# A two-layer attention kernel: one side's key transposes moved from TensorE to VectorE and DMAs, with a new written order

## What is computed

```python
# layer 0: attention, then an MLP
xn, yn = layernorm(x), layernorm(ctx)
q, (k, v) = xn @ Wq, split(yn @ Wkv)                 # 16 heads of 16
x = x + softmax(q k^T * hd**-0.5) v @ Wproj + bproj
x = x + gelu(layernorm(x) @ W1 + b1) @ W2 + b2
# layer 1: the last attention
q = rope(rmsnorm(x) @ wq);  k, v = split(ctx @ wkv);  k = rope(k)
q, k = q / norm(q), k / norm(k)                      # per head
return x + softmax(q k^T * hd**0.5) v @ wout
```

## Time and profile before

| | |
|---|---|
| time, median of 3 runs | 341.33 us (341.09 to 341.97) |
| the profiled execution: its own time | 343.29 us |
| the profiled execution: span | 341.5 us |
| busy: TensorE, VectorE, ScalarE, GpSimd | 97%, 78%, 68%, 57% |
| mean granted TensorE clock | 0.992 |

### The profile page before, as it was taken

How to read it: one execution, slowest core, us unless ns; L and a number is a source line. 1 busy time by engine, 2 the same in 40 slices (tenths; PEclk the granted TensorE clock), 3 DMA queues, 4 the chain that set the end, 5 groups by cost and what they waited for, 6 DMA issues and landing times.

```text
span 341.5 us, 10106 instructions
## 1 busy us (share of the span) xinstructions
PE 330.3 (97%) x3929; PEld 295.5 (87%) x3929; DVE 266.7 (78%) x586; ACT 230.6 (68%) x422; POOL 193.2 (57%) x200
## 2 busy tenths in 40 slices
PE   7899999999999999999999999999998999999995
PEld 7877876888778887899999999999998998888884
DVE  2969989988998669778788788666579989887643
ACT  3568876787775653885736665655678867789871
POOL 3585675886542202635857987493662799647100
PEclk9899999999999999999999999999999999999998
DMA  5667411110020000100000010000000000010101
GB/s 155 200 207 234 138 33 31 33 34 2 3 94 2 3 3 2 33 3 0 3 31 2 0 33 3 31 2 32 2 2 0 3 2 33 17 36 33 50 33 63
DMA packets 13007, 13.79 MB, mean 40 GB/s; under 512 B 1440, under 2 KB 12192, under 8 KB 12960
## 3 DMA queue, kind: packets, MB, share of 16 engines
q1 hardware_dynamic: 12240, 12.34, 11.4%
q10 hardware_dynamic: 720, 0.80, 0.8%
HBM read 11.04 MB, written 2.10 MB: 38 GB/s over the span
## 4 chain that ended last, share of the span: by engine, by line
PE 81%; DVE 6%; issue 4%; POOL 3%; ACT 2%; DMA 1%; ACTq 1%; POOLq 0%; DVEq 0%
PE banks_s L1326 12%; PE bank_y L1121 5%; PE banks_s L1216 5%; PE banks_s L1234 4%; PE banks_s L1393 4%; PE bank_o L1121 4%; PE bank_t L1337 4%; PE bank_y L1337 3%; PE bank_t L1121 3%; PE bank_o L1135 2%; PE bank_y L1135 2%; PE bank_o L1266 2%; PE bank_qk L1337 2%; PE bank_o L1337 2%; DVE row_max L2233 2%
## 5 line engine op out<-in xcount | busy, mean ns | idle before, releaser
L436 POOL TENSOR_TENSOR norm_q_inv<-norm_q_min,minus_half 128x32 f32<-128x32 f32 x8 | 43.8, 5476 | 21.0 <-DVE norm_q_min L2416 19.4
L424 POOL TENSOR_TENSOR norm_k_inv<-norm_k_min,minus_half 128x32 f32<-128x32 f32 x8 | 44.5, 5566 | 12.8 <-DVE norm_k_min L2383 12.7
L659 ACT ACTIVATE PT<-banks_s 128x1024 f32<-128x1024 f32 x32 | 31.0, 1023 | 15.7 <-PE banks_s L1243 15.7
L2233 DVE TENSOR_REDUCE row_max<-banks_s 128x8 f32<-128x1024 f32 x32 | 37.6, 1218 | 4.3 <-PE banks_s L1216 4.0
L703 ACT ACTIVATE W_s<-banks_s,small_t 128x256 f32<-128x256 f32 x60 | 25.2, 471 | 20.1 <-PE banks_s L1326 20.0
L1326 PE MATMUL banks_s<-lnT_hi,W_hi 128*128 128x256 f32 x120 | 34.4, 287 | 0.0
L1326 PE MATMUL banks_s<-lnT_hi,W_lo 128*128 128x256 f32 x120 | 33.9, 283 | 0.0
L1326 PE MATMUL banks_s<-lnT_lo,W_hi 128*128 128x256 f32 x120 | 33.9, 283 | 0.0
L685 ACT ACTIVATE PT<-banks_s 128x1024 f32<-128x1024 f32 x32 | 31.2, 1024 | 3.6 <-PE banks_s L1393 3.6
L712 ACT ACTIVATE hT_hi<-W_s 128x512 fp32r<-128x512 f32 x32 | 20.0, 632 | 15.8 <-PE bank_y L1337 10.1
L389 POOL TENSOR_TENSOR x_all<-x_all,b_row 128x256 f32<-128x256 f32 x16 | 12.4, 794 | 27.2 <-DVE b_xn L2316 25.4
(11 more groups left out here) (375 smaller groups left out, 1088.6 us busy)
## 6 DMA issues: line engine op xcount, KB each, us to landing
x_all<-in_x SPq DMA_DIRECT2D x16, 128.0 KB, 2.2
ctx_in<-in_ctx_wide SPq DMA_DIRECT2D x16, 128.0 KB, 2.5
W_s<-in_L_xattn_W SPq DMA_DIRECT2D x2, 1024.0 KB, 7.8
ctx_in<-in_ctx_T SPq DMA_DIRECT2D x8, 256.0 KB, 2.6
out<-x_all SPq DMA_DIRECT2D x16, 128.0 KB, 1.7
W_s<-in_L_xattn_Wq ACTq DMA_DIRECT2D x1, 256.0 KB, 3.4
W_s<-in_L_xattn_Wkv ACTq DMA_DIRECT2D x1, 256.0 KB, 4.5
W_s<-in_L_xattn_Wkv ACTq DMA_DIRECT2D x2, 128.0 KB, 4.8
```

The costliest lines, as they stand in the source:

```text
L424: nc.gpsimd.tensor_tensor(norm_k_inv[:, :], norm_k_min[:, :], minus_half[:, :], ALU.pow).then_inc(c_kinv, 1)
L436: nc.gpsimd.tensor_tensor(norm_q_inv[:, :], norm_q_min[:, :], minus_half[:, :], ALU.pow).then_inc(c_qinv, 1)
L659: nc.scalar.activation(PT[:, t % 2, 2 * h:2 * h + 2, :], banks_s[:, 2 * h:2 * h + 2, :], ACT.Exp, scale=HD ** -0.5).then_inc(a_exped, 1)
L2233: v.tensor_reduce(row_max[:, 8 * h:8 * h + 8], banks_s[:, 2 * h:2 * h + 2, :].rearrange("p n (r k) -> p (n r) k", k=TOK), AX.X, ALU.max).t ...
```

## The change

1. `keys_T` is gone from TensorE. `keys_blocks` on VectorE transposes each 32x32 square of `rot_k` in one instruction of 128x512 into `key_blocks`, and `move_keys` on SP issues 16 DMAs, each of which takes the squares of one block row and one block column (32 partitions, 4 runs of 128 bytes in each) to their places in `keys_in`. Both tiles lie in `wkv_s`, whose weights have been split by then. `keys_out` and `keys_out_lo` read `keys_in` (SBUF) where they read a bank. `keys_turns(p)` waits for `keys_blocks(p - 1)`, `keys_blocks(p)` for the DMAs of pair p - 1.
2. SP's program: `load_context` runs two pairs ahead of `move_keys`; the stores stand behind all of it.
3. The last tile's end is done in two halves of 8 heads: `out_T_half`, `back_half`, `heads_half`, `normed_half`, `out_hi_half`, `out_lo_half`, `project_half`. `weighted_first(31)` and `weighted_second(31)` write different banks.
4. The three DMAs of `Wkv` are issued by SP behind the first four tile loads, no longer by ScalarE's queue.
5. The written order of all four engines is a new one, with other banks for many results. TensorE turns the first pair after `a_bq`; one more idle transpose stands before `queries_a(0)`.

```diff
@@ SP
             load_ctx(1)
+            sp.dma_start(Wkv_s[:, 0, :], Wkv[0:128, :]).then_inc(wkv_loaded, LOADED)
+            for half in (slice(0, C2B), slice(C2B, 128)):
+                sp.dma_start(Wkv_s[half, 1, :], Wkv[128:C2, :]).then_inc(wkv_loaded, LOADED)
             sp.wait_ge(wkv_loaded, 3 * LOADED)
...
+            def move_keys(p):
+
+                sp.wait_ge(c_kblocks, p + 1)
+                wait(sp, c_keys_lo, p)
+                for a in range(4):
+                    blocks = key_blocks[32 * a:32 * a + 32, :].rearrange("p (n b r) -> p b n r", n=4, b=4)
+                    for b in range(4):
+                        to = keys_in[32 * b:32 * b + 32, :].rearrange("p (n a r) -> p a n r", n=4, a=4)
+                        sp.dma_start(to[:, a], blocks[:, b]).then_inc(c_kmoved, LOADED)
+
+            load_context(0)
+            load_context(1)
             for p in range(NP):
-                load_context(p)
+                if p + 2 < NP:
+                    load_context(p + 2)
+                move_keys(p)
@@ ScalarE
-            def keys_out(p, bank):
-
-                act.wait_ge(c_kT, p + 1)
-                nc.scalar.activation(keysT[:, 0, :, of_pair(p)], joined(bank[:, :]), ACT.Copy).then_inc(c_keys, 1)
+            def keys_out(p):
+
+                act.wait_ge(c_kmoved, 16 * LOADED * (p + 1))
+                nc.scalar.activation(keysT[:, 0, :, of_pair(p)].rearrange("p k (j n) -> p k j n", j=2), keys_in.rearrange("p (j k n) -> p k j n", j=2, k=KT), ACT.Copy).then_inc(c_keys, 1)
@@ TensorE
-            def keys_T(p, bank):
-
-                pe.wait_ge(c_kunit, p + 1)
-                turned_pair(bank, rot_k).then_inc(c_kT, 1)
+            def back_half(h, bank):
+
+                pe.wait_ge(oT_ready, 2 * NB + h)
+                for g in (2 * h, 2 * h + 1):
+                    last = nc.tensor.transpose(bank[:, 128 * g:128 * g + 128], oT[:, 128 * g:128 * g + 128], ident[:, :])
+                last.then_inc(o_back, 1)
+
+            def normed_half(h, bank):
+
+                pe.wait_ge(on_ready, 2 * NB + h)
+                nc.tensor.transpose(bank[:, in_pair(h, TOK)], on[:, in_pair(h, TOK)], ident[:, :]).then_inc(on_transposed, 1)
+
+            def project_half(h, bank):
+
+                pe.wait_ge(onT_lo, 2 * NB + h)
+                for n, (x, y) in enumerate(HI_LO):
+                    last = mm(bank[:, 0:C1], onT_r[:, x, h, :], wout_r[:, y, h, :], start=h == n == 0, stop=h == 1 and n == 2)
+                if h == 1:
+                    last.then_inc(proj_mm, 1)
@@ VectorE
+            def keys_blocks(p):
+
+                dve.wait_ge(c_kunit, p + 1)
+                wait(dve, c_kmoved, 16 * LOADED * p)
+                v.transpose(key_blocks[:, :], rot_k).then_inc(c_kblocks, 1)
```

More of the change, by code:

```diff
@@ new lines, in _ @@
+            pe.wait_ge(c_x_lo, 2)
+            queries_c(1, bank_o)
+            down_b(2, 1, 1, bank_qk)
+            pe.wait_ge(b_gelu, 15)
+            up_b(3, 3, bank_s[0])
+            down_b(2, 1, 2, bank_qk)
+            pe.wait_ge(c_krope, 8)
+            turn_b(4, bank_t)
+            down_b(2, 0, 3, bank_y)
+            down_b(2, 1, 3, bank_qk)
+            pe.wait_ge(c_qrope, 4)
+            keys_c(4, bank_o)
+            pe.wait_ge(b_x, 5)
+            inputs_c(2, bank_y)
+            pe.wait_ge(b_gelu, 16)
@@ L2656, in _ @@
-            res_b(1, 1, bank_y)
             hidden_lo(2, 0)
             hidden_lo(2, 1)
+            res_b(1, 0, bank_qk)
+            queries_units(0)
             hidden_lo(2, 2)
+            keys_out_lo(1)
+            res_b(1, 1, bank_o)
+            inputs_lo(1, bank_o)
+            keys_units(2)
             hidden_lo(2, 3)
-            inputs_lo(1, bank_y)
-            keys_turned(2)
-            keys_sums(2)
-            queries_units(0)
+            hidden_lo(3, 0)
+            keys_blocks(2)
@@ L2680, in _ @@
[L2680 to L2687 removed]
+            split_lnT(4, bank_t)
+            res_b(2, 0, bank_y)
+            res_b(2, 1, bank_qk)
+            centre_b(5)
+            hidden_lo(3, 2)
+            normalise_b(5)
+            inputs_lo(2, bank_y)
+            stats_b(6)
+            hidden_lo(3, 3)
@@ L2707, in _ @@
             keys_units(4)
-            res_b(4, 1, bank_y)
+            normalise_b(7)
+            keys_out_lo(3)
+            res_b(4, 1, bank_t)
+            keys_blocks(4)
             hidden_lo(5, 3)
-            keys_out_lo(4, bank_o)
-            keys_turns(5, bank_y)
+            hidden_lo(6, 0)
+            split_lnT(7, bank_t)
+            keys_turns(5, bank_qk)
+            hidden_lo(6, 1)
             keys_turned(5)
             keys_sums(5)
-            split_lnT(7, bank_o)
-            hidden_lo(6, 0)
@@ L2716, in _ @@
-            hidden_lo(6, 1)
-            res_b(5, 0, bank_t)
+            res_b(5, 0, bank_o)
             hidden_lo(6, 2)
+            res_b(5, 1, bank_y)
+            keys_out_lo(4)
+            hidden_lo(6, 3)
             keys_units(5)
-            keys_out_lo(5, bank_o)
-            keys_turns(6, bank_t)
-            res_b(5, 1, bank_y)
-            hidden_lo(6, 3)
+            keys_blocks(5)
+            queries_out_lo(0, bank_o)
+            queries_out_lo(1, bank_y)
+            inputs_lo(3, bank_o)
@@ L2743, in _ @@
-            heads_out(16, bank_o)
-            keys_turns(7, bank_qk)
-            out_lo(16, bank_o)
-            queries_units(2)
-            queries_sums(3)
-            heads_out(17, bank_o)
+            heads_out(17, bank_qk)
+            queries_turns(4, bank_t)
+            keys_units(6)
+            inputs_lo(5, bank_qk)
+            keys_blocks(6)
+            queries_out_lo(2, bank_y)
+            queries_turned(4)
+            res_b(7, 0, bank_o)
+            queries_sums(4)
+            residual(16, bank_y)
@@ L2759, in _ @@
[L2759 to L2774 removed]
+            inputs_lo(6, bank_y)
@@ L2775, in _ @@
+            queries_turns(5, bank_t)
+            residual(17, bank_o)
+            out_lo(18, bank_y)
+            queries_units(4)
+            keys_out_lo(6)
+            residual(18, bank_o)
+            heads_out(19, bank_qk)
+            queries_turned(5)
+            queries_sums(5)
+            keys_units(7)
+            out_lo(19, bank_o)
+            keys_blocks(7)
+            queries_turns(6, bank_y)
+            heads_out(20, bank_qk)
             inputs_lo(7, bank_o)
-            out_lo(19, bank_t)
@@ L2788, in _ @@
-            out_lo(21, bank_t)
+            queries_out_lo(5, bank_t)
+            out_lo(21, bank_o)
+            keys_out_lo(7)
             heads_out(22, bank_qk)
```

1668 lines of the change are left out of this document (819 added, 849 removed).

## The result

| | before | changed |
|---|---|---|
| median of four runs each, us | 341.33 (341.09 to 341.97) | 347.93 (347.08 to 348.55) |
| ratio to before, 95% interval | 1 | 1.0188 (1.0162 to 1.0215) |
| profiled execution: span, us | 341.5 | 345.3 |
| its own time, us | 343.29 | 347.08 |

The change costs 6.4 us by the ratio; I had forecast 3.5 us of gain and a range up to 341.8. It lies where rival B was, outside the range.

A forecast was written before the change was run, and what follows sets the result against it. TensorE's own issue was taken as the bound from about 30 to about 330 us. Terms -3.5 + 0.3 + 0.1 + 0.5 - 0.5 - 0.4 = -3.5 us gave a median of 337.8 us, range 334.8 to 341.8.

The forecast's parts named there:

- rival B: Moves slower than their room, at `keys_out` on ScalarE; pitch over 0.6, at 0.65 +8 us, so 345.8; chance 0.15.
- TensorE's 32 transposes away: Eight groups of four `keys_T` transposes removed from TensorE, 0.44 us a group, all on the path: -3.5 us.
- VectorE's 8 transposes: Eight added 128x512 instructions at 0.69 us, 5.5 us, mostly covered by VectorE's 28.7 us free: +0.3 us.
- `keys_out_lo` beside GpSimd: With two SBUF inputs on VectorE it may collide with GpSimd's bulk work: 1 us, mostly covered, +0.1 us.
- moves late: ScalarE waits at `keys_out`; about half the pairs late by 1 to 2 us, partly covered: +0.5 us.
- start: TensorE turns the first pair earlier than 11.59 us; gain 1.0 or loss 0.9, taken as -0.5 us.
- end in halves: The last tile's chain after `back`, done in halves, gains 0 to 1 us, taken as -0.4 us.
- new order: New order in every stage; TensorE's list otherwise the same, so only waits change: 0, with +-1.5 us.
- The issue pitch: Time between SP's DMA issues for the moves: 0.475 us taken, bounds 0.475 and 0.94; 16 issues with landing 9.1 us.
- The transposes' worth: TensorE's issue sets the time, so removing eight groups of transposes at 0.44 us each saves 3.5 us.
- a wrong part 1: Signs against the moves: issues over 0.6 us apart, long waits of ScalarE at `keysT` and TensorE for gelu's results.
- The mark for part 4: Sign against the new order's 0 +-1.5 us: TensorE's waits over 10 us in stage a, where no step was removed.

The follow-up runs named there:

- e1: The changed kernel with only the first of each pair's 16 DMAs issued, the other 15 left out; ratio 1.0043, 343.6 us.
- e4: The changed kernel with the three `Wkv` DMAs back on ScalarE's queue; ratio 1.0183.
- e10: The changed kernel with VectorE's `weights_c(0)` and `weights_c(1)` placed behind `maxima(6)` instead of ahead of it; ratio 1.0221.

## Why the prediction was wrong

| step | predicted, us | measured, us |
|---|---|---|
| TensorE's 32 transposes away | -3.5 | -0.7 for 24 of them, where 2.6 would be in proportion |
| VectorE's 8 transposes | +0.3 | +1.9 (+0.95 in the profile) |
| `keys_out_lo` beside GpSimd | +0.1 | no collision |
| moves late | +0.5 | +5.0 and +5.4 |
| start | -0.5 | -0.65 on average in the profiles, by the clock alone |
| end in halves | -0.4 | -0.3 and -0.7, within noise |
| new order | 0 +-1.5 | collisions +2.2 to +3.6 |

**The issue pitch is the step that failed.** The prediction said "I take 0.475, since the queue is otherwise empty in this stage", with bounds of 0.475 and 0.94. It was 0.64, and the issue alone is as long without the other 15 ahead of it, as SP's timeline of `e1` shows:

```profile
233.28 0.59 SPq L310 DMA_DIRECT2D wkv_s<-wkv_s  x1
```

So the shape of the transfer set it, not the traffic. The row of 64 partitions, the nearest in shape, was set aside as traffic. That was half right: the same two issues took 1.88 us before, 2.72 in the changed kernel and 1.11 in `e1`; but even the last is 0.56 each, over my 0.475. And the margin was already negative for the pairs with the least room: my sum had a need of 10.4 us against a room of 7.8 to 13. What the waits cost was the second error of this term: I let delays under 1 us vanish and put +0.5 us for all of them, where ScalarE's 13.0 us of waits cost 5.0. Rival B had the mechanism, the engine, the deciding pitch (over 0.6) and "0.65"; it deserved far more than 0.15. That its 345.8 us came within 2 us of the result is in part luck: its +8 us for the moves was too much, and it knew nothing of the collisions and kept the full -3.5.

**The transposes' worth failed next.** "An instruction taken from it is worth its pitch" held for adding and not for removing. TensorE's timeline has no holes around `keys_T(2)`, but that shows that nothing waits *now*. A TensorE that comes sooner finds others not ready, here GpSimd with the context. VectorE's term failed at one place: its free 28.7 us covered seven of the new instructions nearly, but at pair 6, where TensorE was waiting for VectorE already, all 0.7 us went through. The sizes of both instructions themselves were right: 0.44 us a group and 0.70 against 0.69 us.

**The order was called neutral** since TensorE's list is the same. It is, but the other engines' lists decide who runs beside whom. The number was in sight (1.22 against 0.69 us), looked for in one instruction only.

**Right:** the start, in its size. In the changed kernel the first pair is turned at 10.76 us, not 11.59. At `shifted(0)` this is no longer to be seen: what the new order gains there is that a stretch of slow clock stays away, below, and that was not in my terms. Moving `Wkv`'s queue has no part in it, as `e4` shows.

Of the marks named ahead for a wrong part 1, two appeared: issues further apart than 0.6 us and long waits of ScalarE at `keysT`. The third did not: TensorE waited only 0.7 us for gelu's results, and 1.3 us for `vals_c`. VectorE's transposes and the first turned pair came out right. TensorE's busy time fell by 1.9 us and not 3.5. The mark for part 4, waits over 10 us, was set too high: 3.3 us on `row_max` were enough.

## To carry to other kernels

Price DMA issues by a row of the same shape, and if there is none, take the range's dear end for the case that decides; count issues before bytes. A saving on the busiest engine is worth its full length only if the engines that feed it further on are ready sooner too, so price removal and addition apart, best by a run of each. Where the busiest engine waits for another already, what is added to that other at this place goes through whole, as at pair 6. When an order is rewritten, list which GpSimd instructions with SBUF operands now run beside VectorE's with two of them, and compare the same instruction's duration in both traces before its place is blamed.

## What the runs showed that I had not expected

**A wait can cost twice, through the clock.** TensorE's busy time and granted clock (third column from the right) by stretch, in the profile of the changed kernel with the whole end:

```profile
64.00:68.00 4.00, 1.54 (x21) 0.95 0.19 66
68.00:72.00 4.00, 4.00 (x29) 0.62 0.03 6
72.00:76.00 4.00, 4.00 (x72) 1.00 0.22 66
```

Behind the 2.5 us wait of the first stage the clock falls to its lower level of 1.2 GHz (0.50 in 68 to 70 us) and comes back. `shifted(5)` to `shifted(6)` then takes 9.1 us and not 7.7, 1.4 us more. Of the seven profiles with GpSimd's work at its place in the changed kernel, five show it behind 64 us and `e10` behind its later wait; the changed kernel's own does not. None of the five with `w2_lo_part` moved does. The kernel before has the like at its start: it idles 1.19 us there, and runs like this:

```profile
12.00:16.00 4.00, 4.00 (x24) 0.57 0.63 200
```

Five of the eight profiles in the old order show it and start `shifted(0)` at 27.7 to 28.5 us; the other three do so at 26.8 or 26.9, with no slow stretch. None of the twelve in the new order shows it; they start it at 26.5 to 27.8 us. This is the 1.4 us by which the profiled execution of the kernel before was a poor base for the start. Whether an idle time ends in a slower clock varies from run to run, for the same kernel.

**An issue's length depends on its shape, and not on that alone.** By shape: 0.34 us for a plain block of 128 partitions to device memory, 0.43 for plain loads, 0.60 to 0.65 for 32 partitions in runs of 128 bytes, 0.56 at the least, with single ones up to 1.50 us. But one and the same context load, in the tile view of `ctx_in` before and in the changed kernel, where it stands right behind 16 moves:

```profile
L290 SPq DMA_DIRECT2D ctx_in<-in_ctx_T x8: 367/368/471, 93.9 to 231.5; - x8
L294 SPq DMA_DIRECT2D ctx_in<-in_ctx_T x8: 368/590/591, 99.2 to 243.8; - x8
```

The one difference in sight is what stands ahead in the queue; that it is the cause isn't shown.
